# Moving the whole tail of a six-layer decoder beside its recurrent scan, by token quarters

## The chip, the cores and the metric

The kernel runs on one core of one Trainium2 chip. The metric is the device time of one execution in microseconds (us), the median over several executions.

## What is computed

The input `x` has 4 sequences of 512 tokens with 256 features, and there is a context of the same size. Two decoder layers follow each other, each of three blocks, and after every block stands a layer norm:

```python
x = _layernorm(x + _L0_attn_ref(x, ...))               # gated linear recurrence
x = _layernorm(x + _L0_xattn_ref(x, ctx_1024, ...))    # attention LSTM, 512 steps in order
x = _layernorm(x + _L0_ffn_ref(x, ...))                # first mixture: 8 experts, inner 256, top 2
x = _layernorm(x + _L1_attn_ref(x, ...))               # RWKV-7 scan, 512 steps in order
x = _layernorm(x + _L1_xattn_ref(x, ctx_1024, ...))    # cross attention over all 512 context rows
x = _layernorm(x + _L1_ffn_ref(x, ...))                # second mixture: 4 experts + 1 shared, inner 688, top 2
```

In the LSTM every step attends to the context with its new hidden state, and the attention output goes into the next step's gates. In the RWKV-7 block, state `S` (16 heads of 16x16 for each sequence) is updated token by token:

```python
sa = jnp.einsum('bhij,bhj->bhi', S, a_t)
S = S * jnp.exp(w_t)[:, :, None, :] + sa[..., None] * b_t[:, :, None, :] + v_t[..., None] * k_t[:, :, None, :]
o_t = jnp.einsum('bhij,bhj->bhi', S, r_t)
```

Cross attention, both mixtures and the norms treat each token alone, once the context's keys and values are known.

## The kernel before

All activations stay in SBUF in `xT`: features on partitions (two chunks, `KC` = 2), the 2048 tokens in columns, time-major with the 4 sequences side by side. So 512 columns (`NB`, one block or "quarter") are 128 time steps of all four sequences. The program is a chain of phases; a phase is a `Block` in which each engine has its own instruction stream, ordered by semaphores, and the engines meet at its end.

1. `recurrence_phase`, then `attention_lstm_phase` with a loop of 256 iterations of 2 steps. TensorE sums the gates in PSUM: `half_x` and `half_hid` (input and hidden parts of gates i, f, g for two halves k of the features), then `half_attn(c, k)` (the part of attention chunk c), and `o_gate(u)` (all parts of gate o, into `lstm_ctx_ps`). VectorE transposes each half (`lstm_gates`), ScalarE takes the tanh (`lstm_cell`; `lstm_o_row` for gate o), VectorE makes the cell, transposes the o gate (`lstm_o_col`) and forms `lstm_hid`, with which TensorE starts the scores (`lstm_part_ps` from `lstm_keys`). `lstm_attn` is the attention output, in two chunks, and opens the next step. During the loop SyncE also loads the first mixture's weights, which are all resident (`ResidentWeights`).
2. `mixture_rwkv_phase`. The first mixture of block 0 runs alone. Then comes the scan: `side_by_side` goes over 16 chunks of 32 steps, and after the scan operations of each step (a "slot") each engine draws one piece from a generator that emits the first mixture for blocks 1 to 3. One scan slot is five VectorE operations (`rw_terms`, `rw_sums`, `rw_kept`, `rw_sab`, `rw_state`); the projections for the next chunk of 32 steps are spread over the slots by number: `project_columns` at slot 0 of a chunk (`rw_bank_a` to `rw_bank_c`, TensorE), `project_inner` at 3, `project_gate` at 5, outputs of the chunk before at 22 and 25. `project_columns` waits for `x_done`, an addition that VectorE does at slot 31 of the previous chunk.

   A mixture block has 16 weight chunks of 128 inner rows. For each, TensorE does `gate_up` (two matmul calls into `gate_ps`, two into `up_ps`) and `down` (two calls); ScalarE the silu; VectorE `gated` (`mix_gated`) and `weighted` (`mix_weighted`). At each new expert TensorE also spreads its router weights (`mix_aux_ps`). The generators pause `SLOTS` = 4 slots between chunks:

```python
for c in range(TILES):
    for t in range(STEPS):
        scan_slot(c, t, c + 1 < TILES, c > 0)
        next(mixture, None)
```

3. After the scan: `norm_phase` (all four quarters, with the reciprocal done on 128 columns in quarters), `cross_attention_phase` (a loop over the four sequences, queries and keys of 512 rows each, two sequences overlapped), a norm, `mixture_phase` for the second mixture (5 experts of 6 chunks, 4 blocks each, operands split in a high and a low fp32r part with three passes for each product; GpSimd makes the low parts), and a last norm that stores the output.

## Time and profile before

| | us |
|---|---|
| median of 3 executions | 6856.93 (6853.78 to 6857.31) |
| profiled execution | 6863.35 |
| its span, first to last instruction | 6861.6 |
| LSTM loop | about 252 to 4591 |
| first mixture, block 0 | 4617 to 4740 |
| scan | 4767 to 6039, beside it the first mixture until about 5425 |
| norm, cross attention, norm | 6052 to 6235 |
| second mixture | 6235 to 6832 |
| last norm and store | 6832 to 6861 |

Times in the table's last rows are positions in the span. TensorE is busy in 5571.6 us of the span and VectorE in 3775.7, but the shares change from stage to stage, so each stage has to be read by itself: which engine is nearly always busy in it, or which chain of waits goes round.

### The profile page before, as it was taken

The page shows a single profiled execution, that of the slowest core. Times are in us where ns is not written, and L with a number is a line of the kernel's source. Part 1 is how long each engine was busy: PE and PEld are TensorE (multiplying, and loading weights), DVE is VectorE, ACT ScalarE, POOL GpSimd, SP SyncE. Part 2 cuts the span into 40 slices and gives each one's busy share as a digit, 9 for nine tenths or more (in the row PEclk, how much of TensorE's full clock was granted, in tenths as well). Part 3 has the DMA queues.
Part 4 walks back from the last instruction along what each step waited for, and adds up shares of the span by engine and source line. Part 5 has one row for each costly group of instructions (what it writes and reads, how often), then busy time and mean ns, then how long its engine had stood idle before and what let it go on. Part 6 is the DMA issues. An engine that isn't in the chain of part 4 may idle for free. (4 is left out here: it accounts for less than half of the span.)

```text
span 6861.6 us, 334892 instructions
## 1 busy us (share of the span) xinstructions
PE 5571.6 (81%) x146256; PEld 4143.2 (60%) x146256; DVE 3775.7 (55%) x16432; ACT 1950.4 (28%) x7493; POOL 521.0 (8%) x933
## 2 busy tenths in 40 slices
PE   6888888888888888888888888888777622267998
PEld 3577777777777777777777777764333312135676
DVE  4355555555555555555555555544888999944333
ACT  3133333333333333333333333332121111122211
POOL 0000000000000000000000000000111111111333
PEclk8999999999999999999999999998887765588999
DMA  1200000000000000000000000000000000010000
GB/s 61 87 2 2 2 2 2 2 2 2 2 2 2 2 2 2 2 2 2 2 2 2 2 2 2 2 18 0 0 0 0 0 0 0 0 42 25 13 0 13
DMA packets 25081, 53.02 MB, mean 8 GB/s; under 512 B 5530, under 2 KB 13322, under 8 KB 24358
## 3 DMA queue, kind: packets, MB, share of 16 engines
q1 hardware_dynamic: 23558, 50.96, 2.2%
q10 hardware_dynamic: 1440, 1.06, 0.1%
q8 instruction: 40, 0.66, 0.0%
q14 instruction: 43, 0.35, 0.0%
HBM read 41.48 MB, written 10.52 MB: 8 GB/s over the span
## 5 line engine op out<-in xcount | busy, mean ns | idle before, releaser
L645 PE MATMUL lstm_part_ps<-lstm_keys,lstm_hid 128*4 128x128 f32 x32768 | 989.9, 273 | 280.1 <-DVE lstm_hid L788 280.1
L645 PEld LDWEIGHTS lstm_part_ps<-lstm_keys,lstm_hid 128*4 128x4 f32 x32768 | 823.2, 87 | 416.0 <-DVE lstm_hid L788 398.3
L661 PE MATMUL lstm_ctx_ps<-lstm_values,lstm_alpha 128*4 128x128 f32 x32768 | 988.2, 273 | 0.0
L661 PEld LDWEIGHTS lstm_ctx_ps<-lstm_values,lstm_alpha 128*4 128x4 f32 x32768 | 822.2, 87 | 78.6
L607 PE MATMUL lstm_half_ps<-lstm_w_hid,lstm_hid 128*13 128x96 f32 x16384 | 690.1, 247 | 0.0
L815 DVE TENSOR_REDUCE lstm_neg_max<-lstm_part_ps 128x1 f32<-128x128 f32 x1024 | 298.7, 292 | 546.6 <-PE lstm_part_ps L645 472.4
L755 ACT ACTIVATE lstm_expo<-lstm_part_ps,lstm_neg_max 128x128 f32<-128x128 f32 x1024 | 376.4, 368 | 741.2 <-DVE lstm_neg_max L815 741.2
L607 PE MATMUL lstm_half_ps<-lstm_w_attn,lstm_attn 128*13 128x96 f32 x16416 | 468.1, 248 | 126.5 <-ACT lstm_attn L766 126.5
L840 DVE TENSOR_SCALAR lstm_out_row<-lstm_ctx_ps,lstm_factor 128x128 f32<-128x128 f32 x512 | 179.6, 351 | 579.1 <-PE lstm_ctx_ps L661 579.1
L607 PEld LDWEIGHTS lstm_half_ps<-lstm_w_attn,lstm_attn 128*13 128x13 f32 x16416 | 332.3, 93 | 210.7 <-ACT lstm_attn L766 192.4
L773 DVE STREAM_TRANSPOSE lstm_gates<-lstm_half_ps 128x96 f32<-128x96 f32 x1024 | 230.0, 263 | 391.5 <-PE lstm_half_ps L607 391.5
L856 POOL TENSOR_TENSOR xT<-xT,lstm_attn 128x8 f32 x512 | 105.1, 205 | 4231.4 <-ACT lstm_attn L766 4231.4
L607 PEld LDWEIGHTS lstm_half_ps<-lstm_w_hid,lstm_hid 128*13 128x13 f32 x16384 | 366.6, 94 | 63.1
L762 ACT ACTIVATE lstm_out_row<-lstm_ctx_ps,lstm_factor 128x128 f32<-128x128 f32 x512 | 188.7, 369 | 736.1 <-PE lstm_ctx_ps L661 736.1
L668 PE MATMUL lstm_part_ps<-lstm_ident,lstm_expo 128*128 128x128 f32 x1024 | 336.0, 328 | 43.8
L744 ACT ACTIVATE lstm_cell<-lstm_gates 128x12 f32<-128x12 f32 x1024 | 224.7, 219 | 430.0 <-DVE lstm_gates L773 430.0
L766 ACT ACTIVATE lstm_attn<-lstm_attn_in 128x4 f32<-128x4 f32 x1024 | 214.0, 209 | 424.0 <-DVE lstm_attn_in L844 417.5
L2072 DVE TENSOR_TENSOR rw_terms<-rw_state,rw_sc 128x384 f32<-128x384 f32 x512 | 296.7, 579 | 9.1
L752 ACT ACTIVATE lstm_tanh_c<-lstm_cell 128x4 f32<-128x4 f32 x1024 | 210.2, 205 | 317.4 <-DVE lstm_cell L781 317.4
L607 PE MATMUL lstm_half_ps<-lstm_xg,lstm_masks 128*13 128x96 f32 x8208 | 281.9, 247 | 14.6 <-DMA lstm_xg<-xg_rows 14.6
L668 PEld LDWEIGHTS lstm_part_ps<-lstm_ident,lstm_expo 128*128 128x128 f32 x1024 | 141.6, 138 | 244.1 <-ACT lstm_expo L755 244.1
L844 DVE STREAM_TRANSPOSE lstm_attn_in<-lstm_part_ps 128x32 f32<-128x32 f32 x1024 | 222.2, 217 | 106.4 <-PE lstm_part_ps L674 106.4
(374 smaller groups left out, 9238.6 us busy)
## 6 DMA issues: line engine op xcount, KB each, us to landing
lstm_xg<-xg_rows SPq DMA_DIRECT2D x514, 16.0 KB
xg_rows<-lstm_xg_tile SPq DMA_DIRECT2D x16, 512.0 KB, 2.6
sm_raw_gu<-in_sm_w_gate SPq DMA_DIRECT2D x5, 688.0 KB
sm_raw_gu<-in_sm_w_up SPq DMA_DIRECT2D x5, 688.0 KB
sm_raw_down<-in_sm_w_down SPq DMA_DIRECT2D x5, 575.0 KB
ctxT<-in_ctxT SPq DMA_DIRECT2D x1, 2048.0 KB, 14.7
mix_gu<-in_mix_w_gate SPq DMA_DIRECT2D x8, 256.0 KB, 5.7
mix_gu<-in_mix_w_up SPq DMA_DIRECT2D x8, 256.0 KB, 5.7
```

Source lines behind the costliest of these rows:

```text
L607: mm = pe.matmul(ps[j * STRIP:j * STRIP + ROWS, :], rows, w[:, j * HID + cols.start:j * HID + cols.stop], start=start, stop=stop)
L645: mm = pe.matmul(part_rows(score_ps[part], b), hid[:, k, lo:lo + SPACE], keys[:, k, b * SRC + c * P:b * SRC + (c + 1) * P], start=(n == 0 ...
L661: mm = pe.matmul(part_rows(ctx_ps[o], b), alpha[:, b, c, SPACE - 1 - c:2 * SPACE - 1 - c], values[:, b * SC + c, o * P:(o + 1) * P], start ...
L668: pe.transpose(turned_ps[part], expo[:, part, :], ident[:, :]).then_inc(alpha_turned, 1)
L744: act.activation(cell[:, k, 0:GATES - 1, :], by_batch(turned), ACT.Tanh).then_inc(half_tanh[k], 1)
L752: act.activation(tanh_c[:, k, :], cell[:, k, GATES - 1, :], ACT.Tanh, scale=0.5).then_inc(c_tanh[k], 1)
L755: act.activation(expo[:, part, :], score_ps[part], ACT.Exp, bias=neg_max[:, part:part + 1], accum_out=total[:, part:part + 1]).then_inc(ex ...
L766: act.activation(by_batch(attn[:, o, :]), attn_in[:, o, 0:BATCH], ACT.Tanh).then_inc(attn_ready[o], 1)
L773: dve.transpose(gates[:, k, :], half_ps[k]).then_inc(half_turned[k], 1)
L815: dve.tensor_reduce(neg_max[:, part:part + 1], score_ps[part], AX_X, ALU.max, negate=True)\
L844: dve.transpose(attn_in[:, o, :], attn_ps[o]).then_inc(attn_turned[o], 1)
L2072: dve.tensor_tensor(terms[:, :, :, :], before.unsqueeze(1).to_broadcast([P, 3, HALF, HD]), sc[:, parity, UNIT_KEY:RECV + 1, t, :].unsqueez ...
```

## The change

- **LSTM step**: `o_gate` is cut in two. Its input and hidden parts are issued ahead of the wait for `lstm_attn`, its attention part after the halves. The halves go one after the other (half 0 complete, then half 1), and ScalarE takes the tanh of half 1 after the tanh of cell 0. The LSTM phase loads no mixture weights any more.
- **Tail**: `decoder_tail_phase` takes the place of phases 2 and 3. The list beside the scan (`background`) now holds the first mixture for blocks 1 to 3 (3 slots a chunk) with the four sequences' keys and values after block 1, and then for each quarter `q`, as soon as its tokens have left the scan: norm, cross attention (28 slots), norm, second mixture (68 slots, 2 for each of its 30 chunks) and norm. A quarter's part begins at slot 32 x (4q + 5) at the earliest, so the fourth comes after the scan.
- The second mixture is computed in fp32 in one call for each product, without split operands, in the single-buffered `gate_ps`, `up_ps`, `aux_ps` and `down_ps` that the first one uses; the norms use them too, each for 512 columns with a full-width reciprocal on VectorE.
- Weights of both mixtures are laid out by chunk (gate, up and down of 128 or 115 inner rows: 384 or 358 KB, one DMA) and come through a ring of 6 buffers; the refill of a buffer waits for `down_ready` of its last user. The keys' context goes through the buffers `gu` and `gw`.
- VectorE's `gated` and `weighted` of a chunk stand one whole step behind TensorE's `gate_up` (before: half a step).

```diff
-                        for k in range(KC):
-                            half_attn(0, k)
+                        half_attn(0, 0)
                         pe.wait_ge(attn_ready[1], t + 1)
-                        for k in range(KC):
-                            half_attn(1, k).then_inc(half_ready[k], 1)
-                        o_gate(u)
+                        half_attn(1, 0).then_inc(half_ready[0], 1)
+                        half_attn(0, 1)
+                        half_attn(1, 1).then_inc(half_ready[1], 1)
+                        o_gate_attn()
...
-SLOTS = 4
+SLOTS = 3
+LATE_SLOTS = 2
...
+        def side_by_side(engine, scan_slot, background):
+            for c in range(TILES + 1):
+                for t in range(STEPS):
+                    slot[engine] = c * STEPS + t
+                    scan_slot(c, t, c + 1 < TILES, c > 0)
+                    if c < TILES or t % 4 == 3:
+                        next(background, None)
+            slot[engine] = (TILES + 1) * STEPS
+            for _ in background:
+                pass
+
+        def background(engine, mixture, keys_values, attention):
+            yield from mixture(FIRST, 1, SLOTS)
+            for b in range(BATCH):
+                yield from keys_values(b, SLOTS)
+            yield from mixture(FIRST, 2, SLOTS)
+            yield from mixture(FIRST, 3, SLOTS)
+            for q in range(BLOCKS):
+                yield from until_scanned(engine, q)
+                yield from attention(q, LATE_SLOTS)
+                yield from mixture(SECOND, q, LATE_SLOTS)
...
+            def load_chunk(x, i, n):
+                gn = x.at(i, n)
+                if gn >= RING:
+                    sp.wait_ge(down_ready, gn - RING + 1)
+                width = 2 * KC * x.x.rows + DIM
+                sp.dma_start(ring[:, gn % RING, 0:width], d[f"{x.x.name}_chunks"][n]).then_inc(ring_loaded[gn % RING], 16)
...
+                def gate_up(n):
+                    gn, m, e = x.at(i, n), x.rows(n), x.x.rows
+                    at = gn % RING
+                    pe.wait_ge(ring_loaded[at], 16 * (gn // RING + 1))
+                    if gn > 0:
+                        pe.wait_ge(silu_ready, gn)
+                    for k in range(KC):
+                        mm = pe.matmul(gate_ps[0:m, :], ring[:, at, k * e:k * e + m], token_block(i)[:, k, :],
+                                       start=(k == 0), stop=(k == KC - 1))
...
+                for n in range(3, count):
+                    gate_up(n)
+                    if x.weighted(n) and n % x.x.chunks == 0:
+                        pe.wait_ge(router[x].weight_rows_ready, i + 1)
+                        spread(n)
+                    down(n - 1)
+                    yield from pause(slots)
...
+                for n in range(first_late, x.count):
+                    gated(n)
+                    weighted(n)
+                    yield from pause(slots)
```

On TensorE, one step of the LSTM (the second of an iteration) stood so before; `lstm_half_ps` are gates i, f, g, `lstm_ctx_ps` from 13 rows is gate o:

```order
L674 MATMUL lstm_part_ps<-lstm_out_row,lstm_masks 4x32 x4
L685 REGISTER_ALU
L607 MATMUL lstm_half_ps<-lstm_w_attn,lstm_attn 13x96 x16
L607 MATMUL lstm_ctx_ps<-lstm_xg,lstm_masks 13x64 x4
L607 MATMUL lstm_ctx_ps<-lstm_w_hid,lstm_hid 13x64 x8
L607 MATMUL lstm_ctx_ps<-lstm_w_attn,lstm_attn 13x64 x8
```

and stands so now:

```order
L679 MATMUL lstm_part_ps<-lstm_out_row,lstm_masks 4x32 x4
L608 MATMUL lstm_ctx_ps<-lstm_xg,lstm_masks 13x64 x4
L608 MATMUL lstm_ctx_ps<-lstm_w_hid,lstm_hid 13x64 x8
L691 REGISTER_ALU
L608 MATMUL lstm_half_ps<-lstm_w_attn,lstm_attn 13x96 x16
L608 MATMUL lstm_ctx_ps<-lstm_w_attn,lstm_attn 13x64 x8
```

Twelve calls of the o gate have gone ahead of the sixteen that need the attention output.

On VectorE, beside the scan, one chunk of the first mixture stood so before, with 20 scan operations in four slots up to the next chunk's `mix_gated`; here its two own operations and the slot between them:

```order
L2095 TENSOR_TENSOR mix_gated<-mix_gated,mix_up_ps 128x512
L2072 TENSOR_TENSOR rw_terms<-rw_state,rw_sc 128x384
L2077 TENSOR_REDUCE rw_sums<-rw_terms 128x16
L2079 TENSOR_TENSOR rw_kept<-rw_terms,rw_vk 128x128
L2081 TENSOR_TENSOR rw_sab<-rw_sums,rw_sc 128x128
L2086 TENSOR_TENSOR rw_state<-rw_kept,rw_sab 128x128
L2103 TENSOR_TENSOR mix_weighted<-mix_gated,mix_aux_ps 128x512
```

and a chunk of the second mixture, which was in no scan before, stands so now (a second slot of the same five rows follows before the next `mix_gated`):

```order
L2074 TENSOR_TENSOR mix_gated<-mix_gated,mix_up_ps 115x512
L2087 TENSOR_TENSOR mix_weighted<-mix_gated,mix_aux_ps 115x512
L2049 TENSOR_TENSOR rw_terms<-rw_state,rw_sc 128x384
L2054 TENSOR_REDUCE rw_sums<-rw_terms 128x16
L2056 TENSOR_TENSOR rw_kept<-rw_terms,rw_vk 128x128
L2058 TENSOR_TENSOR rw_sab<-rw_sums,rw_sc 128x128
L2063 TENSOR_TENSOR rw_state<-rw_kept,rw_sab 128x128
```

So two scan slots, no longer four, separate one chunk's pair from the next.

## Rows read from the trace of the kernel before

**Rows 1.** The page's first line.
```profile
span 6861.6 us, 334892 instructions
```

**Rows 2.** Windows: start:end, us, busy PE PEld DVE ACT POOL (instructions), PEclk, DMA, GB/s.
```profile
4767.00:5411.00 644.00, 483.93 (x1368) 241.94 (x1366) 557.25 (x1422) 136.93 (x245) 77.69 (x97) 0.85 0.00 0
5425.00:6038.00 613.00, 147.59 (x652) 117.63 (x650) 578.85 (x1523) 75.23 (x162) 86.87 (x110) 0.60 0.00 0
...
6076.00:6205.00 129.00, 114.01 (x320) 56.59 (x320) 29.16 (x56) 44.33 (x99) 12.06 (x8) 0.94 0.10 33
...
6235.00:6832.00 597.00, 562.26 (x2272) 409.36 (x2272) 208.12 (x342) 112.54 (x173) 215.68 (x146) 0.96 0.03 11
```

**Rows 3.** Lines of VectorE, 4768 to 5411: count, busy us, mean ns, idle before.
```profile
L2072 DVE TENSOR_TENSOR rw_terms<-rw_state,rw_sc 128x384 f32<-128x384 f32 x231 | 130.6, 565 | 2.8
...
L2095 DVE TENSOR_TENSOR mix_gated<-mix_gated,mix_up_ps 128x512 f32<-128x512 f32 x48 | 32.6, 680 | 66.9 <-PE mix_up_ps L1752 66.9
```

**Rows 4.** Timeline, 5086 to 5140: start us, length us, engine; TensorE and VectorE.
```profile
5114.98 3.75 PE L1671 MATMUL rw_bank_a<-rw_x_in,rw_w_r 128*128 128x128 f32 x16 [4.68 <-DVE xT L2058]
...
5128.00 1.88 PE L1745 MATMUL mix_gate_ps<-xT,mix_gu 128*128 128x512 f32 x4
...
5131.71 0.69 DVE L2095 TENSOR_TENSOR mix_gated<-mix_gated,mix_up_ps 128x512 f32<-128x512 f32 x1 [8.68 <-PE mix_up_ps L1752]
```

**Rows 5.** Timeline, one LSTM step, 3011 to 3015.
```profile
3011.55 0.21 ACT L766 ACTIVATE lstm_attn<-lstm_attn_in 128x4 f32<-128x4 f32 x1 [0.67 <-DVE lstm_attn_in L844]
...
3011.82 0.88 PE L607 MATMUL lstm_half_ps<-lstm_w_attn,lstm_attn 128*13 128x96 f32 x32 [0.22 <-ACT lstm_attn L766]
3011.92 0.21 ACT L766 ACTIVATE lstm_attn<-lstm_attn_in 128x4 f32<-128x4 f32 x1 [0.15 <-DVE lstm_attn_in L844]
...
3012.60 0.45 DVE L773 STREAM_TRANSPOSE lstm_gates<-lstm_half_ps 128x96 f32<-128x96 f32 x2 [0.72 <-PE lstm_half_ps L607]
...
3012.80 0.28 PEld L607 LDWEIGHTS lstm_ctx_ps<-lstm_w_attn,lstm_attn 128*13 128x13 f32 x16
...
3013.32 0.22 ACT L748 ACTIVATE lstm_o_row<-lstm_ctx_ps 128x64 f32<-128x64 f32 x1 [0.18 <-PE lstm_ctx_ps L607]
...
3013.58 0.20 ACT L752 ACTIVATE lstm_tanh_c<-lstm_cell 128x4 f32<-128x4 f32 x1
3013.58 0.24 DVE L809 STREAM_TRANSPOSE lstm_o_col<-lstm_o_row 128x64 f32<-128x64 f32 x1
3013.93 0.17 DVE L788 SCALAR_TENSOR_TENSOR lstm_hid<-lstm_o_col,lstm_tanh_c 128x4 f32<-128x4 f32 x1
```

**Rows 6.** Timeline, 4650 to 4665: TensorE from one chunk of block 0 to the next.
```profile
4659.21 1.88 PE L1745 MATMUL mix_gate_ps<-xT,mix_gu 128*128 128x512 f32 x4
...
4664.36 1.02 PE L1745 MATMUL mix_gate_ps<-xT,mix_gu 128*128 128x512 f32 x2
```

**Rows 7.** Timeline, 4997 to 5025: VectorE, first and last of a router's 13 operations.
```profile
5005.45 0.18 DVE L1063 COPY mix_router_logits<-mix_aux_ps 128x32 f32<-128x32 f32 x1
...
5009.42 0.19 DVE L1085 TENSOR_TENSOR mix_router_weights<-mix_router_weights,mix_router_total 128x32 f32<-128x32 f32 x1
```

**Rows 8.** Timeline, 4720 to 4742: the 512-column norm after block 0.
```profile
4725.48 1.98 PE L93 MATMUL mix_gate_ps<-xT,mean_mat 128*128 128x512 f32 x4 [1.32 <-DVE xT L2124]
...
4733.84 3.35 DVE L118 RECIPROCAL mix_out_ln_rstd<-mix_out_ln_rstd 128x512 f32<-128x512 f32 x1 [5.12 <-ACT mix_out_ln_rstd L113]
4737.23 1.23 DVE L120 TENSOR_TENSOR xT<-mix_out_ln_d,mix_out_ln_rstd 128x1024 f32<-128x1024 f32 x1
```

**Rows 9.** Timeline, 6036 to 6062: from the scan's end to its last output.
```profile
6039.19 0.29 DVE L2148 TENSOR_REDUCE rw_sums<-rw_terms 128x8 f32<-128x128 f32 x1
...
6050.27 0.60 DVE L2058 TENSOR_TENSOR xT<-xT,rw_bank_a 128x256 f32<-128x256 f32 x1 [7.22 <-PE rw_bank_a L1720]
```

**Rows 10.** DMA issues: KB each, median us to landing.
```profile
mix_gu<-in_mix_w_gate SPq DMA_DIRECT2D x8, 256.0 KB, 5.7
...
out_xT<-xT SPq DMA_DIRECT2D x4, 512.0 KB, 3.1
```

More of the change, by code:

```diff
@@ L1565, in mixture_rwkv_phase @@
         gw = s.sb("mix_weighted", [P, 2, NB])
+        ring = s.sb("mix_ring", [P, RING, RING_W])
+        keys = s.sb("ca_keys", [P, KC, BATCH * SRC])
+        values = s.sb("ca_values", [P, BATCH * SC, DIM])
+        queries = s.sb("ca_queries", [P, KC, NB])
+        neg_max = s.sb("ca_neg_max", [P, BATCH])
+        total = s.sb("ca_total", [P, BATCH])
+        ctx = (gu, gw)
+        prob, prob_t = gu, gw
         gate_ps = s.ps("mix_gate_ps", [P, NB])
@@ new lines, in mixture @@
+                router[x].keep_logits(act, i, (b_router if x is FIRST else no_bias)[:, :])
+                silu(0)
+                yield from pause(slots)
+                if not x.weighted(0):
+                    silu(1)
+                router[x].keep_expo(act, i)
+                yield from pause(slots)
+                router[x].keep_rows(act, i)
+                for n in range(1 if x.weighted(0) else 2, x.count):
+                    silu(n)
+                    yield from pause(slots)
@@ L1907, in _ @@
             act.wait_ge(loaded, 16 * LOADS)
-            for _ in mixture(range(0, 1), 1):
+            act.wait_ge(zeroed, 3)
+            for _ in mixture(FIRST, 0, 1):
                 pass
@@ L2086, in scan_slot, with mixture, gated @@
                 dve.tensor_tensor(after, kept[:, :, :], sab[:, :, :], ALU.subtract).then_inc(state_ready, 1)
-            def mixture(blocks, slots):
-                early, late = slots - slots // 2, slots // 2
-                def gated(i, n):
-                    gn = i * CHUNKS + n
+            def mixture(x, i, slots):
+                block_x = token_block(i)
+                def gated(n):
+                    gn, m = x.at(i, n), x.rows(n)
+                    at = gn % 2
                     dve.wait_ge(silu_ready, gn + 1)
@@ new lines, in mixture @@
+                yield from pause(slots)
+                gated(0)
+                yield from pause(slots - 1)
+                router[x].vector(dve, i)
+                yield
+                if x.weighted(0):
+                    yield from pause(slots - 1)
+                    weighted(0)
+                    yield
+                    first_late = 1
+                else:
+                    first_late = 1
+                for n in range(first_late, x.count):
+                    gated(n)
+                    weighted(n)
+                    yield from pause(slots)
@@ L2416, in on_partitions, with by_chunk @@
     return np.ascontiguousarray(b.reshape(-1, P).T)
-def each(f, ws):
-    return np.ascontiguousarray(np.stack([f(w) for w in ws]))
+def by_chunk(x, gate, up, down):
+    out = np.zeros((len(x.order) * x.chunks, P, 2 * KC * x.rows + DIM), np.float32)
+    for n in range(len(out)):
+        e, lo, m = x.order[n // x.chunks], (n % x.chunks) * x.rows, x.rows_of(n % x.chunks)
+        for which, w in enumerate((gate, up)):
+            for k in range(KC):
+                at = (which * KC + k) * x.rows
+                out[n, :, at:at + m] = w[e][k * P:(k + 1) * P, lo:lo + m]
+        out[n, 0:m, 2 * KC * x.rows:] = down[e][lo:lo + m]
+    return out
 def by_quarter(w):
```

1044 lines of the change are left out of this document (405 added, 639 removed).

## The prediction

> **What bounds the kernel now.** I read the page, then windows of busy time cut at the phases, then in each stage the waits and the timeline. The span is 6861.6 us [rows 1]; no engine bounds all of it.
>
> In the LSTM a chain goes round through four engines, so only what lies on it counts. The reader should follow one step [rows 5]: attention chunk 1 is there at 3011.92 + 0.21 = 3012.13, the gates are transposed from 3012.60, the o gate's last weight load starts its 16 calls' halves at 3012.80 and ends at 3013.08, `lstm_o_row` starts at 3013.32, `lstm_o_col` at 3013.58, `lstm_hid` at 3013.93.
>
> In the scan VectorE is the bound. Without a mixture beside it, 277 slots (233 or so of 512 lie before) take 613 us, 2.21 us each, with VectorE busy for 579 of them [rows 2]. With it, 231 slots take 644 us [rows 2, 3]; of these VectorE waits 66.9 us for `up_ps` [rows 3]. The reader should see why [rows 4]: at slot 0 of each 32 TensorE must do `project_columns`, from 5114.98 to 5128.00, 13.0 us, and only then `gate_up`, so VectorE gets its next product at 5131.71, 16.7 us after the lump began, having waited 8.7.
>
> After the scan, 822 us remain, 597 of them the second mixture, where TensorE is busy for 562 [rows 2].
>
> **LSTM, step by step.** The o gate's 24 input and hidden loads go into the gap ahead of the attention output. At 0.28 us for 16 [rows 5] they take 0.42, and the gap is about as long, so half 0's first eight calls may start 0.1 late; but its second eight wait for chunk 1 at 3012.13 anyway. Half 0 is unchanged, half 1 about 0.14 later (eight more loads ahead), which VectorE, busy with the first transposition, mostly hides. Behind chunk 1 stand now 24 + 16 loads and not 16 + 40 less those under way: the o gate ends 0.20 us earlier, `lstm_o_row` too. `lstm_o_col` can't gain all of it, since VectorE makes the cell just before, and `lstm_hid` needs tanh of the cell, at 3013.58 + 0.20 and a semaphore, 3013.82. So `lstm_hid` moves from 3013.93 to 3013.82: 0.11 us on 512 steps, **56 us gained**. Bounds: 0 if the loads ahead delay half 0 by as much, 0.20 x 512 = 102 if cell and tanh move too. I take 56.
>
> **VectorE in the scan.** Costs of the first mixture's work: 32 operations of 0.68 [rows 3], a router of 4.1 (5005.45 to 5009.61) [rows 7], an addition of about 1.2 and a norm of 1.2 + 3.35 + 1.2 [rows 8]: 33 us a block. From 644 take 66.9 of waits and 92 of such work: 485 / 231 = 2.10 us for a slot of its own. The new scan has 512 of them, 1075 us. Added: 3 x 33 = 99 for the first mixture as before; and for each of three quarters 54 operations of 0.68 = 37, router 4, addition 1.2, three norms 17.4 and some 6 for the maxima and the attention's addition (near the norm's rows): 65.5, together 196. VectorE alone: **1371 us**, against 1272 now.
>
> **TensorE in the scan.** A chunk in fp32 takes 4664.36 - 4659.21 = 5.15 us for six calls [rows 6], 0.86 each; partitions (115 or 128) don't enter, columns do. Projections: 147.6 us busy in 277 slots [rows 2], 17 per 32 slots, 13.0 of them in the lump. First mixture, 3 slots a chunk: TensorE 5.15 + 0.4 + 1.6 = 7.2, VectorE 6.3 + 1.4 = 7.7. VectorE stays the bound, but at each lump it waits as in rows 4, some 8.5 us, 6.3 times = 54; keys and values (two times four calls' worth, 7 us a sequence, behind a context load that starts only at `ln_done`, as long as a 256 KB load or more [rows 10]) stand ahead of a lump and cost about 12. So 201 slots: 422 + 99 + 54 + 12 = **587 us**.
>
> Second mixture, 2 slots a chunk: VectorE 4.2 + 1.4 = 5.6, TensorE 5.15 + 0.1 + 1.1 = 6.3: **TensorE becomes the bound**. For the 62 slots with chunks: 30 x 5.15 + 4 x 0.86 + router about 5 + projections 33 = 197, and 8 for the restart after two lumps, since they begin only when VectorE has reached slot 31: 205. The third quarter has a period without projections: 187. So 597 for three. The norm behind it, 6 slots: 12.6 + 5.8 = 18.4, three times 55. The attention part, 28 slots: 58.8 + 17 + 5 of waits = 81, three times 243. 23 slots are idle between the second and third quarter, 51. Sum 946, and the scan **1533 us, 261 more**. Bounds: 1371 (TensorE fully hidden, -162), and about 1650 (a lump's whole 16.7 us lost 15 times in place of 8.5).
>
> The Trainium skill, page "FP8 and Floating Point Precision", section "TensorE Precision Notes", says true fp32 makes four passes through the array. Before, the second mixture made three passes in fp32r, so by that rule a chunk's matmuls grow by a third: from 562 / 120 = 4.7 us [rows 2] to 6.2, as an estimate. The trace has fp32 chunks themselves, at 5.15 [rows 6], which is less; I go by them. By the page the scan's 90 chunks would cost 95 us more and the last 30 another 32.
>
> **The tail.** Only quarter 3 is left. Last outputs 6039.0 to 6050.9 [rows 9]: 12. Norm 4725.48 to 4738.46, 13.0 [rows 8], 15 with TensorE at its lower level: the clock was 0.60 in the scan without a mixture [rows 2]. Attention: 129 / 4 = 32 us for a sequence, keys and values in it [rows 2], those (7) fall away, but two sequences overlapped there and nothing does here: 35. Norm 14. Mixture: 154.5 + 3.4 + 6 = 164, last additions 5, norm 13, store 512 KB, 3.1 to landing and some [rows 10], 5. Sum **263**, against 822: 560 gained (rounded). Bounds 240 to 300.
>
> **The start.** Seven more loads hide behind the norm. The first ring load starts when the block does, while the router's logits are summed: 2 us lost. Nothing else loads in the LSTM: no effect. Ring loads in the steady state: 358 to 384 KB every 6 us, five chunks (30 us) ahead, against 5.7 us for 256 KB [rows 10]: hidden.
>
> **Sum.** 6861.6 + 261 - 560 - 56 + 2 = 6509. The profiled execution took 1.75 more than its span and lies 6.4 above the median: **6504 us**.
>
> **Rivals.**
> 1. *VectorE stays the only bound*; one more step of distance between `gate_up` and `gated` lets TensorE's lumps hide. For it: 16.7 us are not much more than two steps of 7.7; against it: TensorE's own sum in the late chunks is above VectorE's. 6504 - 162 = **6342**; half of it 6420.
> 2. *The LSTM gains nothing*: the early o loads push the halves. For it: the gap ahead of 3011.82 is as short as the loads. **6560**; if they cost 0.1 a step, 6610.
> 3. *The lower clock beside the scan, and slower than before.* All 90 second-mixture chunks in the scan with TensorE at half clock take 5.15 more each: 6504 + 464 = **6968**. It decides from 69 chunks (353 / 5.15). For it: the clock was 0.85 with TensorE busy 484 of 644 us [rows 2], and it was 0.60 in the sparse stretch. Against it: TensorE's busy share rises here from 75 to above 90 per cent, and where TensorE was busy for 94 per cent (562 of 597) the clock was 0.96 [rows 2]. The Trainium skill, page "TensorE: Matmul & The Clock Gate", section "Why this matters for your kernels", warns that idle gaps between matmul bursts send the array back to half rate; the stretch at 0.60 agrees. By that rule the fuller TensorE holds the upper level, so it speaks for the forecast.
> 4. *The ring does not keep up*, so weights are not hidden as the change says: if loads went one after another at 5.7 us for 256 KB, a chunk took 8.3: 90 x 2.0 + 30 x 3.2 = 276, **6780**. Against it: six are in flight.
>
> **How the numbers follow.** Forecast (6440 to 6590) 0.60; rival 1 below 6440, 0.19; rival 2, from 6560 up with the scan as forecast or worse, 0.13; rival 3, 0.04, of it 0.03 slower than before; rival 4, 0.04. For 8 in 10 I go from halfway into rival 1, 6390, to 6620. A change under 0.2% (14 us) is what a measurement of this kernel can't tell from none. Faster 0.96, same 0.01, slower 0.03.
>
> **What would show it.** LSTM: the loop 56 us shorter, `lstm_hid` 0.11 closer to the attention tanh. Scan: 1533 us from first to last `rw_terms`; VectorE waiting for `mix_up_ps` in all second-mixture chunks, at about 6.3 us a chunk; TensorE's clock at 0.95 or more there. Tail: 263 us from the last `rw_terms`, chunks at 5.15. I would be wrong if VectorE hardly waits, if late chunks take over 7 us, or if TensorE waits for DMA of `mix_ring`.

## The result and the profile after

The changed kernel takes **6506.9 us** (6506.4 to 6508.8, four executions) against 6857.1 in the same session: ratio 0.9491, 95% interval 0.9474 to 0.9507, so 350 us or 5.1% faster. The prediction said 6504. A sum that comes out within 3 us can still be made of errors that cancel, so the parts matter more than the total.

The page's first line, against [rows 1]:

```profile
span 6504.8 us, 332594 instructions
```

The step boundaries come from the view of one tile (operation, count, shortest, median and longest duration in ns, first and last start):

```profile
L773 ACT ACTIVATE lstm_attn<-lstm_attn_in x1024: 208/209/214, 266.0 to 4543.9; 128x4 f32<-128x4 f32 x171
...
L2049 DVE TENSOR_TENSOR rw_terms<-rw_state,rw_sc x512: 493/553/1080, 4718.7 to 6243.1; 128x384 f32<-128x384 f32 x171
```

For the kernel before the same views give 267.5 to 4590.9 and 4767.4 to 6036.7. The span splits at the last attention tanh of the LSTM, the scan's first product and its last:

| stretch | before | after | difference | predicted |
|---|---|---|---|---|
| up to the LSTM's last tanh | 4590.9 | 4543.9 | -47.0 | -56 |
| from there to the scan's first `rw_terms` | 176.5 | 174.8 | -1.7 | +2 |
| first to last `rw_terms` | 1269.3 | 1524.4 | +255.1 | +261 |
| from there to the end (the tail) | 824.9 | 261.7 | -563.2 | -560 |
| span | 6861.6 | 6504.8 | -356.8 | -353 |

Windows of the new scan, in the columns of [rows 2]: slots 0 to 200 (first mixture, keys and values), quarter 0's norm and attention (slots 201 to 228), its 62 slots with chunks (229 to 290), the same stretch run on to slot 293, the idle stretch before quarter 2, the whole scan, and the tail:

```profile
4718.70:5301.60 582.90, 473.35 (x1383) 239.23 (x1381) 507.02 (x1260) 137.52 (x237) 64.75 (x83) 0.90 0.12 36
5301.60:5386.30 84.70, 53.12 (x206) 32.44 (x206) 72.94 (x171) 23.16 (x47) 8.73 (x11) 0.77 0.00 1
5386.33:5577.31 190.98, 186.47 (x516) 86.10 (x516) 166.82 (x418) 43.27 (x72) 21.71 (x27) 0.98 0.16 47
5386.30:5590.60 204.30, 199.76 (x568) 95.39 (x569) 172.57 (x432) 48.02 (x84) 22.48 (x28) 0.98 0.15 44
5905.20:5957.00 51.80, 4.95 (x20) 4.29 (x21) 49.87 (x131) 2.70 (x7) 7.05 (x9) 0.50 0.17 53
4718.70:6244.30 1525.60, 1235.54 (x3667) 621.27 (x3665) 1318.11 (x3248) 359.26 (x634) 165.60 (x210) 0.90 0.12 35
6244.30:6504.80 260.50, 208.32 (x526) 89.50 (x526) 71.72 (x103) 44.09 (x72) 4.13 (x6) 0.91 0.15 47
```

In the 62 slots with second-mixture chunks TensorE is busy for 186.5 of 191.0 us, at a granted clock of 0.98; VectorE for 166.8. Over the whole scan VectorE is the fuller one, 1318 of 1526. In the idle stretch the clock falls to 0.50, and nobody waits for TensorE there.

What VectorE waits for in the scan (waiting line, releaser: us in all, times, longest), where [rows 3] had 66.9 in one row:

```profile
DVE mix_gated L2074 <- PE mix_up_ps L1558: 58.5, 27, 10.2
DVE tail_ln_rstd L121 <- ACT tail_ln_rstd L116: 22.8, 3, 9.5
DVE xT L2106 <- PE mix_down_ps L1573: 14.7, 2, 7.4
DVE mix_weighted L2077 <- PE mix_up_ps L1558: 14.1, 4, 5.9
DVE rw_kk_norm L1982 <- ACT rw_kk_sq L1745: 12.9, 1, 12.9
DVE mix_weighted L101 <- PE mix_gate_ps L96: 11.8, 4, 6.8
DVE rw_kk_norm L1993 <- ACT rw_kk_norm L1760: 10.4, 1, 10.4
```

All of VectorE's waits in the scan add up to 154 us. The rest of the scan, 1524 - 154 = 1370, is called VectorE's own here: the 1318 us in which it is busy and some 52 us of gaps too short for the view of waits. How a wait comes about is seen at the projection lump of slot 256, the first that meets quarter 0's chunks (timeline, as in [rows 4]):

```profile
5469.12 1.95 PE L1472 MATMUL rw_bank_a<-rw_x_in,rw_w_r 128*128 128x128 f32 x16
...
5478.18 1.89 PE L1472 MATMUL rw_bank_c<-rw_w_v,rw_x_in 128*128 128x256 f32 x8
...
5479.90 1.88 PE L1547 MATMUL mix_gate_ps<-xT,mix_ring 128*115 128x512 f32 x4
...
5481.62 1.88 PE L1558 MATMUL mix_up_ps<-xT,mix_ring 128*115 128x512 f32 x4
...
5483.61 0.69 DVE L2074 TENSOR_TENSOR mix_gated<-mix_gated,mix_up_ps 115x512 f32<-115x512 f32 x1 [10.24 <-PE mix_up_ps L1558]
...
5491.71 0.69 DVE L2074 TENSOR_TENSOR mix_gated<-mix_gated,mix_up_ps 115x512 f32<-115x512 f32 x1 [3.21 <-PE mix_up_ps L1558]
```

The lump runs from 5469.1 to 5479.9, only then gate and up of the next chunk; VectorE has nothing else left and waits 10.2, and 3.2 once more for the next chunk. Most chunks between lumps show no waits: from 5504.1 to 5545.5 seven chunks follow each other, 5.9 us each, and VectorE waits for nothing there, since two scan slots, a chunk's own pair and the operations of the projection keep it busy longer than a chunk's 5.15 us (and 0.86 at a new expert) keep TensorE. Where no operation of the projection falls to VectorE, a chunk takes it only 4.8 us (5431.5 to 5436.3), less than TensorE's 5.15, and there small waits do appear: 0.2 and 0.3 us in slots 251 and 253, and 0.4, 1.2 and 0.3 in slots 281 to 285.

The attention LSTM, two steps in a row (as [rows 5]):

```profile
3011.64 0.29 PE L608 MATMUL lstm_ctx_ps<-lstm_xg,lstm_masks 128*13 128x64 f32 x8
...
3012.14 0.21 ACT L773 ACTIVATE lstm_attn<-lstm_attn_in 128x4 f32<-128x4 f32 x1 [0.15 <-DVE lstm_attn_in L851]
...
3012.83 0.61 DVE L780 STREAM_TRANSPOSE lstm_gates<-lstm_half_ps 128x96 f32<-128x96 f32 x2 [0.72 <-PE lstm_half_ps L608]
...
3014.03 0.17 DVE L795 SCALAR_TENSOR_TENSOR lstm_hid<-lstm_o_col,lstm_tanh_c 128x4 f32<-128x4 f32 x1
...
3020.34 0.30 PE L608 MATMUL lstm_ctx_ps<-lstm_xg,lstm_masks 128*13 128x64 f32 x8 [0.23 <-issue]
...
3020.42 0.21 ACT L773 ACTIVATE lstm_attn<-lstm_attn_in 128x4 f32<-128x4 f32 x1
...
3021.30 0.61 DVE L780 STREAM_TRANSPOSE lstm_gates<-lstm_half_ps 128x96 f32<-128x96 f32 x2 [0.91 <-PE lstm_half_ps L608]
...
3022.50 0.17 DVE L795 SCALAR_TENSOR_TENSOR lstm_hid<-lstm_o_col,lstm_tanh_c 128x4 f32<-128x4 f32 x1
```

In the first, the early o gate starts at 3011.64, well ahead of the attention tanh (3012.14), and `lstm_hid` comes 1.89 after that tanh (2.01 in [rows 5]). The second is the first step of a loop iteration: the early calls start only at 3020.34 after an idle time marked "issue", the gates are transposed 0.88 after the tanh and not 0.69, `lstm_hid` comes 2.08 after it. So steps alternate between 8.28 and 8.465 us; before they alternated between 8.40 and 8.485.

### The profile page after: what moved, and what is told of

Read it like the earlier page. It is cut to its first block and busy times, and to the rows that moved or that the text cites. A ratio compares the mean times of both kernels' runs of the same rounds, so it can differ in the third digit from the quotient of the medians.

```text
span 6504.8 us, 332594 instructions
## 1 busy us (share of the span) xinstructions
PE 5746.6 (88%) x145488; PEld 3981.4 (61%) x145488; DVE 3742.4 (58%) x16358; ACT 2001.6 (31%) x7480; POOL 290.9 (4%) x779
## 5 line engine op out<-in xcount | busy, mean ns | idle before, releaser
L780 DVE STREAM_TRANSPOSE lstm_gates<-lstm_half_ps 128x96 f32<-128x96 f32 x1024 | 289.8, 283 | 441.1 <-PE lstm_half_ps L608 417.2
L608 PE MATMUL lstm_half_ps<-lstm_w_attn,lstm_attn 128*13 128x96 f32 x16416 | 501.5, 247 | 1.4 <-ACT lstm_attn L773 0.7
L1558 PE MATMUL mix_up_ps<-xT,mix_ring 128*128 128x512 f32 (+2 forms) x736 | 360.0, 613 | 38.2 <-DVE mix_gated L2074 35.8
L1573 PE MATMUL mix_down_ps<-mix_weighted,mix_ring 128*128 128x512 f32 (+2 forms) x736 | 358.5, 611 | 9.7 <-DVE mix_weighted L2087 9.7
L1808 ACT ACTIVATE mix_gated<-mix_gate_ps 128x512 f32<-128x512 f32 (+2 forms) x184 | 109.9, 597 | 811.0 <-PE mix_gate_ps L1547 801.7
L1547 PE MATMUL mix_gate_ps<-xT,mix_ring 128*128 128x512 f32 (+2 forms) x736 | 358.9, 611 | 0.0
L608 PE MATMUL lstm_half_ps<-lstm_xg,lstm_masks 128*13 128x96 f32 x8208 | 305.7, 249 | 8.7 <-DMA lstm_xg<-xg_rows 8.7
```

The source lines that it names most:

```text
L608: mm = pe.matmul(ps[j * STRIP:j * STRIP + ROWS, :], rows, w[:, j * HID + cols.start:j * HID + cols.stop], start=start, stop=stop)
L780: dve.transpose(gates[:, k, :], half_ps[k]).then_inc(half_turned[k], 1)
L1547: mm = pe.matmul(gate_ps[0:m, :], ring[:, at, k * e:k * e + m], token_block(i)[:, k, :], start=(k == 0), stop=(k == KC - 1))
L1558: mm = pe.matmul(up_ps[0:m, :], ring[:, at, lo:lo + m], token_block(i)[:, k, :], start=(k == 0), stop=(k == KC - 1))
L1573: mm = pe.matmul(down_ps[:, o_, :], ring[0:m, gn % RING, lo + o_ * P:lo + (o_ + 1) * P], gw[0:m, gn % 2, :], start=(n == 0), stop=(n == co ...
```

## The experiments

Times are medians; all are to be held against 6857 and 6507. The experiments ran in four sessions, and the kernel before, run again in each, came out between 6856 and 6862, so a few us between runs of different sessions show nothing.

**The LSTM order undone.**

```diff
-                        o_gate_x_hid(u)
                         pe.wait_ge(attn_ready[0], t + 1)
-                        half_attn(0, 0)
+                        for k in range(KC):
+                            half_attn(0, k)
                         pe.wait_ge(attn_ready[1], t + 1)
-                        half_attn(1, 0).then_inc(half_ready[0], 1)
-                        half_attn(0, 1)
-                        half_attn(1, 1).then_inc(half_ready[1], 1)
+                        for k in range(KC):
+                            half_attn(1, k).then_inc(half_ready[k], 1)
+                        o_gate_x_hid(u)
                         o_gate_attn()
```

ScalarE's tanh of half 1 goes back too, ahead of the tanh of cell 0 (not shown).

> The changed kernel with the LSTM step's TensorE and ScalarE order of before; everything else as changed, so still no mixture weights loaded in the LSTM. Reading of the two traces: after the first step a step alternates between 8.40 and 8.485 us before, 8.28 and 8.465 now, so the order is worth 256 x 0.12 + 256 x 0.02 = 36 us, and 8.3 us came from the first step alone (16.73 against 8.4), which this kernel keeps: about 6543. The prediction's term (0.11 us a step, all of it from the order): 6563. Rival (the order gains nothing): 6507.

Measured: 6543.5. The order is worth 36.6 us. The other 8.3 us of the LSTM's 45 come from one step. In the kernel before, the second step's input row stood on SP's queue behind the 24 transfers of mixture weights, and TensorE waited (timeline of the kernel before, step 1):

```profile
276.81 0.83 PE L607 MATMUL lstm_half_ps<-lstm_xg,lstm_masks 128*13 128x96 f32 x16 [5.95 <-DMA lstm_xg<-xg_rows]
```

From `lstm_out_row` to `lstm_out_row` that step took 16.73 us (266.47 to 283.20); without those loads the first step takes what the others take.

**The lump in three pieces.** The columns stay at slot 0 of each 32, the four row products follow at slots 2 and 4, and what depends on them two or three slots later:

```diff
+            def project_rows(m, n):
...
                 if has_next and t == 0:
                     project_columns(c + 1)
-                if has_next and t == 3:
+                if has_next and t in (2, 4):
+                    project_rows(c + 1, t // 2 - 1)
+                if has_next and t == 6:
                     project_inner(c + 1)
```

> The projection lump of TensorE at slot 0 of each 32 is cut in three pieces, at slots 0, 2 and 4, and what follows from it goes two or three slots later. Theory A (beside the second mixture TensorE's sum of work is the bound, the lump's delay is not): VectorE's waits for up_ps vanish beside the first mixture (24 us) and at the norms of the attention parts (17 us), but the 62 slots with second-mixture chunks still take about 204 us: 6465. Theory B (it is the delay of one lump that VectorE waits for, everywhere): 85 us of waits go, those beside the second mixture too: about 6422. If the lump doesn't matter: 6507.

Measured: 6472.4, 34.5 us less, near theory A's 6465. The largest waits of VectorE in this scan:

```profile
DVE mix_gated L2086 <- PE mix_up_ps L1563: 41.7, 24, 3.7
DVE rw_kk_norm L1994 <- ACT rw_kk_sq L1754: 23.3, 4, 18.6
DVE tail_ln_rstd L121 <- ACT tail_ln_rstd L116: 18.0, 5, 8.6
```

Beside the first mixture the waits for `up_ps` nearly go. Beside the second the one wait of 10.2 and one of 3.2 become four of 3.3, 3.7, 3.7 and 2.1: the same 13 us. Cutting the lump doesn't help where TensorE has well under 1 us to spare in each chunk (5.9 against 5.15, before the spreads); there its sum over the lump and the chunks around it decides. The 62 slots with chunks took 193.3 us in quarter 0, against 191.0.

**Idle slots used, scattered.** Every third chunk of quarters 0 and 1 gets a third slot:

```diff
+        def rest(x, i, n, slots):
+            return pause(slots + (1 if x is SECOND and i < 2 and n >= 5 and n % 3 == 2 else 0))
```

> Every third chunk of the second mixture of quarters 0 and 1 gets 3 slots in place of 2 (9 each), which uses 18 of the 23 slots that stand idle before quarter 2. Theory A (TensorE's sum is the bound in these stretches, 204 us for 62 slots): the stretches stay at about 206 us with 71 slots in them, and 18 slots of 2.25 go from the idle stretch: 36 us less, 6471. Theory B (only the delay of the lump costs): each of the 18 slots costs VectorE the same wherever it stands: 6507.

Measured: 6508.0, no change: theory A fails here. Quarter 0's chunks, spread over 71 slots, took 216.7 us and not 206. VectorE's waits add up to 155 us as before, at other places: 8.4 in place of 13.4 at slot 259, but 10.3 in place of 7.4 at slot 291, and so again in quarter 1 (10.4 and 9.3 for 13.5 and 7.4), the rest in new waits of 1 to 2 us.

**Keys and values 7 slots later.** One line, `yield from pause(7)`, ahead of the keys in `background`. The changed kernel's timeline there:

```profile
4899.69 3.67 PE L1638 MATMUL mix_gate_ps<-mix_gated,ca_w_k 128*128 128x512 f32 x4 [13.20 <-DMA mix_gated<-in_ctxT]
...
4910.73 2.05 PE L1472 MATMUL rw_bank_a<-rw_x_in,rw_w_r 128*128 128x128 f32 x16 [2.19 <-ACT rw_x_in L1732]
...
4922.78 0.42 DVE L1982 TENSOR_REDUCE rw_kk_norm<-rw_kk_sq 128x16 f32<-128x256 f32 x1 [12.88 <-ACT rw_kk_sq L1745]
...
4941.98 0.25 DVE L1993 RECIPROCAL rw_kk_norm<-rw_kk_norm 128x16 f32<-128x16 f32 x1 [10.39 <-ACT rw_kk_norm L1760]
```

TensorE waits 13.2 us for the context, whose load is issued only at 4895.2, behind the norm, then does the first sequence's keys and values, and the projection lump starts at 4910.7, 13.7 us after VectorE made its input (4896.4 and 0.6); VectorE waits 12.9 and 10.4 for the two steps behind it.

> Keys and values start 7 slots later, behind the projection of slots 64 to 68; the following work is 7 slots later, which the 23 idle slots take up. Theory (the 23.3 us that VectorE waits for rw_kk_sq and rw_kk_norm at slots 69 and 73 come from the context load and the four keys-and-values pieces that stand ahead of the projection on TensorE and ScalarE): 15 to 20 us less, 6490. Rival (the same work collides with whatever comes next, first-mixture chunks that wait for k_kept, so that the wait only changes its name): 6507.

Measured: 6530.9, 24 us slower. Waits of VectorE in this scan:

```profile
DVE mix_gated L2075 <- PE mix_up_ps L1559: 119.2, 52, 10.0
...
DVE rw_kk_norm L1983 <- ACT rw_kk_sq L1746: 9.2, 3, 3.5
```

The waits at the keys went from 23.3 to 5.8 us, as expected. But everything after them stands 7 slots later against the lumps, which now meet chunks where they met norms: the waits of `mix_gated` went from 58.5 to 119.2, and all waits to 183 us.

**Idle slots used, at the lumps.** The same `rest`, but 4 extra slots for a chunk of these two quarters that starts in slot 0 or 1 of 32, and for no other:

```diff
+        def rest(engine, x, i, slots):
+            at_lump = x is SECOND and i < 2 and slot[engine] % STEPS in (0, 1)
+            return pause(slots + (4 if at_lump else 0))
```

> As in the run before with idle slots, 16 of the 23 idle slots go to the second mixture of quarters 0 and 1, but now four at a time and only to the chunk that TensorE starts right behind a projection lump (slots 257 and 289, and the two that answer to them in quarter 1). Theory (the scan is VectorE's own 1370 us plus its waits, and a wait of 10 us is made by each lump that meets a chunk of two slots): the four places' waits (10.2 + 3.2 and 7.4, twice, 41.6 us) go, about 36 us less after small new ones: 6471. Rival (slots handed out do nothing, as when they were scattered, since TensorE's sum comes back as a wait elsewhere): 6507.

Measured: 6492.6, 14.3 less, between the two.

```profile
DVE mix_gated L2078 <- PE mix_up_ps L1562: 37.4, 24, 4.8
DVE rw_kk_norm L1986 <- ACT rw_kk_sq L1749: 26.2, 5, 12.9
...
DVE ca_total L2131 <- ACT mix_gated L1848: 7.5, 1, 7.5
```

The 41.6 us at the four places are gone; in their place VectorE now reaches `rw_kk_sq`, a step of the projection itself, before the lump is done (13.4 us in four places), and quarter 1's attention meets a lump (7.5 in `ca_total`, 4.8 beside it).

**Half the contraction.** In the second mixture gate and up multiply only one of the two feature chunks:

```diff
+                    ks = 1 if x is SECOND else KC
-                    for k in range(KC):
+                    for k in range(ks):
```

> Leaves out half of the second mixture's gate and up products (the second of the two feature chunks is not multiplied), so a chunk's matmuls take 3.4 us and not 5.15; VectorE's and ScalarE's work is unchanged. Tail: 30 x 1.72 = 52 us less by every theory. Scan, by the theory of waits made by lumps: TensorE catches up faster, of the 85 us of waits beside the second mixture and its norms some 30 go: 6425. By rival 1 of the prediction (with TensorE out of the way VectorE alone bounds the scan beside the late chunks, only the 50 us of waits ahead of slot 201 stay): 6355. If TensorE's sum bounded all the late stretches: 3 x (204 - 174) = 90 us less, 6365.

Measured: 6421.8, 85 us less, where waits made by lumps gave 82. The scan is 1487.3, 37 less, although TensorE's busy time in it is 111 less (1235.5 to 1124.1); the tail is 49.5 less. The 62 slots with chunks went from 191.0, 191.3 and 188.0 us to 180.9, 179.9 and 175.3 in the three quarters.

```profile
DVE mix_gated L2075 <- PE mix_up_ps L1559: 28.7, 13, 4.8
```

So rival 1's bound isn't reached by a faster TensorE either: 118 us of waits stay, for the lump, 10.8 us long, is still there.

**A ring of three buffers** (`RING = 3`).

> The ring has 3 buffers and not 6. A chunk's load lands 2.9 to 3.0 us after its issue, and a refill is now issued about one chunk (5.15 us or more) ahead of its use. My theory: no change, 6507. By rival 4 of the prediction (loads one after another, 8.3 us a chunk) this would cost over 200 us; if a load comes 1 us late in each of the 30 chunks of the tail and a part of the others: 6540.

Measured: 6508.7, no change. A load lands 2.9 to 3.0 us after its issue (last column, page of the changed kernel), and with three buffers TensorE waits for the ring three times from the scan on, 3.9 us in all:

```profile
mix_ring<-in_sm_chunks SPq DMA_DIRECT2D x120, 358.0 KB, 2.9
mix_ring<-in_mix_chunks SPq DMA_DIRECT2D x64, 384.0 KB, 3.0
```

**Four LSTM steps in an iteration** (`UNROLL = 4`).

> Four steps of the LSTM in an iteration of its loop, not two. In the changed kernel the second step of an iteration takes 8.28 us and the first 8.465, in which TensorE idles 0.23 us ahead of the early o gate at the loop's edge. Theory (the edge costs the 0.19): 128 edges fewer, 24 us less, 6483. Rival (the two steps differ by their place in the buffers, not by the edge): 6507.

Measured: 7459.1, 952 us slower. Three of four steps take 8.28 us, as expected, but once per iteration TensorE stands still (timeline):

```profile
3026.53 0.29 PE L608 MATMUL lstm_ctx_ps<-lstm_xg,lstm_masks 128*13 128x64 f32 x8
...
3038.49 0.30 PE L608 MATMUL lstm_ctx_ps<-lstm_xg,lstm_masks 128*13 128x64 f32 x8 [3.50 <-issue]
...
3041.62 0.50 PE L608 MATMUL lstm_ctx_ps<-lstm_w_hid,lstm_hid 128*13 128x64 f32 x9 [2.72 <-issue]
```

The page shows what it waits for. DMA queue of instructions, packets, MB and share, first of the changed kernel, then of this one:

```profile
q8 instruction: 45, 0.74, 0.0%
```

```profile
q8 instruction: 1446, 23.69, 1.4%
```

So with four steps instructions are fetched over and over, 23 MB more or 179 KB an iteration, and each iteration takes 952 / 128 = 7.4 us longer; with two steps the whole program brings 0.74 MB onto this queue. The bytes and the standstill came together; no run takes them apart. The Trainium skill, page "Runtime: NRT & Kernel Launch", section "Instruction fetch mechanics", says that a taken branch whose target has left the two pages that an engine holds has to fetch it by DMA before it goes on; the bytes and the 3.5 and 2.7 us of "issue" agree. It adds that kernels prefer full unrolling where possible; going part of the way, from two to four steps, made this loop slower.

**The loop's edge moved.** TensorE's loop is rotated: the gates of the next step stand at the end of an iteration, those of the first ahead of the loop.

```diff
+                gates(0, 1)
                 with pe.Fori(0, SEQ // UNROLL) as i:
                     for u in range(UNROLL):
...
-                        o_gate_x_hid(u)
-                        pe.wait_ge(attn_ready[0], t + 1)
...
-                        o_gate_attn()
...
                         select(1)
+                        gates(nxt, t + 2)
```

> The changed kernel with TensorE's loop in the LSTM rotated: the gates of the next step (early o gate, attention parts) stand at the end of an iteration and not at its head, the first step's ahead of the loop, so the loop's edge meets the wait for the transposed halves. Theory (the 0.19 us between the two steps of an iteration are the edge's cost on TensorE, and after the attention tanh nothing hides it): 256 x 0.19 = 48 us less, 6459. Rival (another engine's edge, or the place in the buffers): 6507.

Measured: 6463.7, 43.2 less, near the 48 expected. All steps now take 8.28 to 8.29 us.

**The lump in three pieces, and slots beside it.** The two together, with one extra slot for each chunk of quarters 0 and 1 that starts in slots 0 to 13.

> The lump in three pieces, and beside it one extra slot for every second-mixture chunk of quarters 0 and 1 that starts in slots 0 to 13 of a chunk of 32 (some 18 of the 23 idle slots). Theory (the scan is VectorE's own 1365 us plus waits, and an idle slot moved to a stretch where TensorE is behind takes up to 2.1 us of waits away): against the lump in three pieces alone (6472) up to 38 us, less a third for new waits where quarter 1 now meets its lumps: 6445. Rival (extra slots only rename the waits): 6472.

Measured: 6493.8, 21 us slower than the three pieces alone.

```profile
DVE rw_kk_norm L1998 <- ACT rw_kk_sq L1758: 64.4, 9, 18.9
DVE rw_kk_norm L2009 <- ACT rw_kk_norm L1773: 23.8, 3, 12.9
DVE mix_gated L2090 <- PE mix_up_ps L1567: 21.4, 18, 3.3
```

The waits for `up_ps` halved, from 41.7 to 21.4, and those for `rw_kk_sq` and `rw_kk_norm` went from 34.3 to 88.2. With two more chunks let in between the pieces, the lump of slot 352 ends 21 us after it began, and VectorE, no longer held up by chunks, reaches the projection's next step 13.2 us early. The wait has changed its name, and grown.

**Edge, three pieces, keys 7 slots later, extra slots in slots 0 to 7 only.**

> The rotated LSTM loop, the lump in three pieces, keys and values 7 slots later, and extra slots for chunks in slots 0 to 7 only. By the waits' account: 48 (edge) and 17 (VectorE's waits at the keys) and some 15 (extra slots) less than the lump in three pieces alone: 6392. If later keys cost by a shifted schedule what they did alone (24 us more): 6435.

Measured: 6426.6. That is 46 less than the three pieces alone, of which the edge makes 43: the other two edits gave 3, not 32, and 3 us is within what sessions differ by. VectorE's waits are 121 us, against 129.

**The norms' reciprocals off VectorE**, on top of the last kernel:

```diff
-        act.activation(self.rstd[:, :], self.var_ps, ACT.Sqrt, bias=eps).then_inc(self.std_ready, 1)
+        act.activation(self.rstd[:, :], self.var_ps, ACT.Ln, bias=eps).then_inc(self.std_ready, 1)
+        act.wait_ge(self.std_ready, n + 1)
+        act.activation(self.rstd[:, :], self.rstd[:, :], ACT.Exp, scale=-0.5).then_inc(self.rstd_ready, 1)
...
-        dve.reciprocal(self.rstd[:, :], self.rstd[:, :]).then_inc(self.rstd_ready, 1)
```

> The kernel of the run before (edge, lump in three, slots, later keys: 6427), with the tail's 16 full-width reciprocals (3.35 us each on VectorE) gone: ScalarE makes exp(-0.5 ln(var + eps)) in place of the root, two operations of about 0.7 us and a table load or two, and VectorE only multiplies. Theory (in the scan each microsecond of VectorE's own work is a microsecond of the kernel, except where it meets a wait for TensorE): 12 norms stand in the scan, 12 x 3.4 = 41 us less of VectorE's own work, 1368 to 1327, and 5 us from the four norms with nothing beside them: 6381 if the waits stay at 121, about 6405 if half of it comes back as waits for TensorE. Rival (TensorE bounds the late stretches as the prediction had it, so that only the first mixture's three norms count): 6412.

Measured: 6397.4 (ratio to before 0.9331, interval 0.9316 to 0.9347), 29 less than the kernel it builds on and the fastest of all. The tile's view shows two operations of 0.69 and 0.63 us on ScalarE, where one of 0.69 stood, and no reciprocal on VectorE ([rows 8] had 3.35). A table load of 1.28 us stands between the two, so ScalarE's part takes 2.6 us from start to end (6385.6 to 6388.2):

```profile
L120 ACT ACTIVATE tail_ln_rstd<-mix_up_ps,eps x16: 687/687/688, 4638.3 to 6385.6; 128x512 f32<-128x512 f32 x16
L122 ACT ACTIVATE tail_ln_rstd<-tail_ln_rstd x16: 629/629/631, 4640.3 to 6387.6; 128x512 f32<-128x512 f32 x16
L126 DVE TENSOR_TENSOR xT<-mix_weighted,tail_ln_rstd x16: 1216/1225/1226, 4640.9 to 6388.3; 128x1024 f32<-128x1024 f32 x16
```

The scan went from 1489.4 to 1465.9 us. VectorE's own part fell by 38.6 (1367.9 to 1329.3), as worked out, and its waits grew by 15 (121.5 to 136.6): two fifths came back. The tail is 5 us shorter. None of these norms stands among the slots with chunks: from the norm ahead of them to the addition behind them the three quarters took 215.2, 213.2 and 189.3 us, against 214.8, 213.2 and 188.5.

## Why the prediction was right, and where only its total was

**The account that holds.** In nine of ten kernels the scan, less all of VectorE's waits (summed over the whole view), is the same within 9 us, and in the tenth it is shorter by the work taken out. (The ring of three, the four steps and the moved edge, which leave the scan as it is, are not in the table; they give 1370 to 1372.)

| kernel | scan | waits | VectorE's own |
|---|---|---|---|
| changed | 1524.4 | 154.3 | 1370.1 |
| LSTM order undone | 1524.8 | 155.7 | 1369.1 |
| lump in three | 1489.7 | 128.7 | 1361.0 |
| slots scattered | 1524.1 | 154.7 | 1369.4 |
| keys later | 1552.1 | 183.4 | 1368.7 |
| slots at lumps | 1507.5 | 139.6 | 1367.9 |
| half contraction | 1487.3 | 117.6 | 1369.7 |
| three pieces and slots | 1510.8 | 144.6 | 1366.2 |
| edge, pieces, slots, keys | 1489.4 | 121.5 | 1367.9 |
| the same, norms off VectorE | 1465.9 | 136.6 | 1329.3 |

The prediction's "VectorE alone: 1371 us" was right to 1 us. What it added, 162 us, was measured as 154, but it was placed wrongly: that the scan came out at 1524 for 1533 is in part luck.

**LSTM, 56 predicted, 47 measured** (1.5 of it from an earlier start). The term was mis-sized: 0.11 us a step was taken for all, and the runs give 0.12 for the second step of an iteration and 0.02 for the first, 36.6 by the run without the new order. What ate the rest is the loop's edge, which the prediction didn't look at: an iteration's first step took 0.085 us more than its second before and takes 0.185 more now, and moving the edge gave 43 us. "Nothing else loads in the LSTM: no effect" failed; the loads' removal was worth 8.3 us. Rival 2 (no gain) is dead.

**Slots 0 to 200, 587 predicted, 583 measured.** Two errors cancel. The first mixture's lumps were put at 54 us and cost 28. A lump that meets chunks now makes two waits, 4.7 to 7.0 us together, where [rows 4] had one of 8.7. Two things changed at once. One more step of distance between `gate_up` and `gated` may absorb part of a lump, which was rival 1's mechanism. And the lumps themselves are shorter. Windows of the lump of [rows 4] and, in the changed kernel, of one beside the first mixture (columns as in [rows 2]):

```profile
5115.00:5128.00 13.00, 13.00 (x64) 11.78 (x65) 7.75 (x18) 0.00 (x0) 0.00 (x0) 0.82 0.00 1
```

```profile
5002.00:5012.70 10.70, 10.70 (x65) 9.61 (x64) 9.32 (x23) 0.00 (x0) 0.00 (x0) 1.00 0.13 38
```

Before, four of the seven lumps between slots 32 and 224 came after TensorE had stood idle for 4.0 to 8.6 us; they took 12.4 to 13.6 us at a granted clock of 0.80 to 0.86, and VectorE waited 8.1 to 11.7 for each. The other three took 10.8 to 10.9 at 1.00, and the waits were 3.3, 6.5 and 6.5. The prediction took its 8.5 from the first kind, and all lumps of this stretch are now of the second. No run took the two causes apart, so how much each gave is open. Keys and values were put at 12 and cost 23, because the context load is waited for ahead of the lump.

**Second mixture beside the scan, 652 predicted with its norms, 635 measured.** The 62 slots with chunks were put at 205, 205 and 187 us and took 191.0, 191.3 and 188.0; the six slots behind them, with the last addition and a norm, were put at 18.4 and took 26.8, 26.8 and 12. "TensorE becomes the bound", with VectorE waiting in every chunk at 6.3 us, is the step that failed as stated. The two sums behind it were good. From quarter 0's first gate product (5388.4) to the end of its last down product (5586.4) TensorE takes 198.0 us; the prediction had 197 (its terms add up to 196) and 8 more for restarts. VectorE's own part of the 62 slots is 174, 191.0 less 17.0 of waits, which is the prediction's 5.6 a chunk. VectorE meets the 24 us between the two as a few waits behind the lumps, 17.0 in the slots and 7.4 for the last down product behind them. From this trace alone that could still be read as a TensorE bound; two runs speak against it. Nine more slots beside the same chunks should then have been free (206 us), but the stretch took 216.7. And with a third of the matmuls of these chunks left out, 111 us of TensorE's busy time in the scan, the scan should have lost 90 and lost 37. (The run with the norms off VectorE gained where the norms stand and says nothing of the slots with chunks.) So neither engine is the bound alone: each is ahead for a while, and only a lump makes VectorE wait for long. Rival 1 (VectorE alone, 6342) is wrong by these waits. The sign that the prediction named, a wait in every second-mixture chunk, is absent: there are 22 waits for `up_ps` beside 90 chunks.

**Attention, 243 predicted, 255 measured; idle stretch 51 and 51.8.** The 12 us are lumps that meet the norms (waits of 9.5, 7.8 and 5.6 for `tail_ln_rstd`, and one of 6.8 at a norm's start): the waits of the three parts add up to 30, where the prediction had 5 each.

**Tail, 263 predicted, 261.7 measured**, and chunks at 5.15 us as [rows 6] gave. The total is closer than its parts: the last outputs took 18.6 us where 12 was forecast, the attention 30.3 for 35, the mixture 168.4 for 164, the last addition 1.2 for 5, and the errors cancel. A pair of 512-column calls takes 1.72 us, 0.86 each, which is 4 x 512 columns at 2.4 GHz. The Trainium skill, page "FP8 and Floating Point Precision", section "TensorE Precision Notes", says four passes; the trace agrees. Its use in the prediction, a third on top of 562 / 120 us, gave 6.2 and was wrong, since 4.7 us a chunk also held router and spreading. The 18 calls of a chunk alone took 4.18 us before (6402.36 to 6406.54), and a third on top of that is 5.57, still above 5.15; why is open.

**Rival 3, the clock.** It was 0.98 beside the second mixture. It was 0.77 in quarter 0's attention, where TensorE was busy for 53 of 85 us, and 0.50 in the idle stretch, where it was busy for 5 of 52. **Rival 4, the ring**: half of it is enough.

**What stays open.** How the lumps should stand against the chunks. Of the runs that changed how the two meet and left the work as it is, only the lump in three pieces came out near its forecast (42 us, 34.5 measured). Of the runs that moved slots, the forecasts were 36, 17, 36, 27 and 32 us and the gains 0, -24, 14, -21 and 3: the waits that a shift makes were read from the trace afterwards, never worked out ahead. A kernel with keys and values behind slot 75 (in the fastest kernel VectorE still waits 13 us for `rw_kk_norm` there) wasn't tried.

## What to carry to other kernels

Where work is laid beside a serial scan, add up the scan engine's own work and keep its waits in a separate account: the first stayed within 11 us in twelve kernels here, the second depends on which slot meets which lump of the other engine, and moves whenever anything is shifted. Cutting work on the pacing engine returned 23 us of 39; using idle slots returned 0, 14 and -21 us where 36, 36 and 27 were expected. In a loop of 8 us per step, look at where its edge stands and what stands ahead of the first loads on the queue: the edge was worth 43 us, more than the 36.6 of the reordering, and the queue 8.3.

## What the hardware showed beside this

- A loop body of four LSTM steps brings 23.7 MB onto the instruction queue where one of two steps has 0.74, and the loop takes 7.4 us an iteration more.
- The edge of TensorE's loop cost 0.17 to 0.19 us (43.2 / 256 by the run, 8.465 - 8.28 by the trace) when it stood right ahead of work that nothing hides, and nothing when it stood ahead of a wait.
- The same lump of 64 matmul calls took 10.7 us at a granted clock of 1.00 and 12.4 to 13.6 at 0.80 to 0.86, where TensorE had stood idle for 4.0 to 8.6 us before it.
- ScalarE makes the inverse root as a logarithm and an exponential in 0.69 + 0.63 us for 128x512 with a table load of 1.28 us between them, 2.6 us in all, against 0.69 us for its root and 3.35 us for VectorE's reciprocal of the same tile. The Trainium skill, page "ScalarE: Activation LUTs", section "What it computes", names VectorE's reciprocal with a root for this; where VectorE paces the kernel, the run with the other form was 29 us faster.
